# Routed experts of a mixture layer: rows padded to 64 instead of 128 per expert, with pair tiles that hold two experts

## The reference

```python
logits = x @ gate_weight.T                      # 2048 tokens, 8 experts
scores = softmax(logits)
topk_w, topk_idx = top_k(scores, 2)             # two experts per token
gu  = einsum('th,efh->tef', x, gate_up_weights) # 512 -> 2 * 352
act = silu(gu[..., :352]) * gu[..., 352:]
y   = einsum('tef,te,ehf->th', act, combine, down_weights)   # 352 -> 512
y   = y + shared expert (704 wide, all tokens)
```

## Time and profile before

| | |
|---|---|
| time, median of 3 runs | 2844.9 us (2841.21 to 2847.65) |
| profiled execution, its own time | 2848.35 us |
| span of its trace | 2846.3 us |
| mean granted TensorE clock | 0.986 of full speed |
| PE busy (TensorE products) | 2768.9 us, 97% of the span, 13041 records |
| VectorE, ScalarE, GpSimd busy | 1754.0, 1222.0, 607.7 us |
| span of the expert tiles on TensorE | 615.2 to 951.2 us of the span |

### The profile page before, as it was taken

How to read it: one execution, slowest core, us unless ns; L and a number is a source line. 1 busy time by engine, 2 the same in 40 slices (tenths; PEclk the granted TensorE clock), 3 DMA queues, 4 the chain that set the end, 5 groups by cost and what they waited for, 6 DMA issues and landing times. The chain is left out here.

```text
span 2846.3 us, 37554 instructions
## 1 busy us (share of the span) xinstructions
PE 2768.9 (97%) x13041; PEld 1558.3 (55%) x13042; DVE 1754.0 (62%) x4334; ACT 1222.0 (43%) x2268; POOL 607.7 (21%) x669
## 2 busy tenths in 40 slices
PE   8999999989999988999999999999999999999998
PEld 3444444436565445666666656666666665664432
DVE  5767762011111276777877778777787778645986
ACT  4646431012122145456545565455655555342243
POOL 1111101401111312133123331333213332120000
PEclk9999999999999988999999999999999999999999
DMA  3101134031221652011100111001120011227313
GB/s 134 50 1 44 45 114 180 23 122 63 66 66 62 231 219 78 16 46 68 68 30 31 43 63 75 31 31 42 54 85 31 31 42 49 75 75 262 126 48 104
DMA packets 78501, 215.22 MB, mean 76 GB/s; under 512 B 12128, under 2 KB 13056, under 8 KB 69760
## 3 DMA queue, kind: packets, MB, share of 16 engines
q1 hardware_dynamic: 58704, 165.84, 16.0%
q0 software_dynamic: 9264, 28.36, 3.1%
q10 hardware_dynamic: 10368, 18.88, 1.8%
HBM read 156.25 MB, written 56.80 MB: 75 GB/s over the span
## 5 line engine op out<-in xcount | busy, mean ns | idle before, releaser
L2477 DVE SCALAR_TENSOR_TENSOR c_conv<-c_ps_pj,c_conv_t,c_conv 128x511 f32<-128x511 f32 (+2 forms) x450 | 336.2, 747 | 30.0 <-ACT c_conv L2296 19.4
L1961 POOL TENSOR_SCALAR c_gate<-c_gate 128x512 f32<-128x512 f32 x64 | 37.9, 620 | 997.1 <-DVE c_block_L L2510 997.1
L2036 PE MATMUL c_ps_pj<-c_xs,c_w_v 128*128 128x512 f32 x480 | 225.8, 593 | 0.0
L2036 PE MATMUL c_ps_pj<-c_xs,c_w_q 128*128 128x512 f32 x360 | 177.0, 614 | 0.0
L2057 PE MATMUL c_ps_pj<-c_w_g,c_xs 128*128 128x512 f32 x384 | 172.7, 592 | 0.0
L2036 PE MATMUL c_ps_pj<-c_xs,c_w_k 128*128 128x512 f32 x360 | 164.7, 593 | 0.0
L2296 ACT ACTIVATE c_conv<-c_ps_pj,c_conv_t 128x512 f32<-128x512 f32 x150 | 116.6, 777 | 56.3 <-issue 27.6
L1284 DVE TENSOR_TENSOR x_act<-x_hs,x_ps_u 128x352 f32<-128x352 f32 x40 | 20.9, 521 | 191.6 <-ACT x_hs L1269 191.6
L2359 ACT ACTIVATE c_err<-c_negL 32x128 f32<-32x128 f32 x256 | 79.1, 309 | 135.1 <-DVE c_negL L2543 130.4
L2507 DVE TENSOR_TENSOR c_block_X<-c_block_X,c_block_t 128x58 f32<-128x58 f32 (+6 forms) x448 | 117.7, 263 | 15.4
L2504 DVE TENSOR_TENSOR c_block_t<-c_block_L,c_block_X 128x58 f32<-128x58 f32 (+6 forms) x448 | 117.6, 263 | 14.9
(11 more groups left out here) (587 smaller groups left out, 5962.8 us busy)
## 6 DMA issues: line engine op xcount, KB each, us to landing
c_xs<-xt_d SPq DMA_DIRECT2D x16, 1024.0 KB, 4.8
c_G<-cum_d SPq DMA_DIRECT2D x16, 1024.0 KB, 4.6
ot_d<-c_oT ACTq DMA_DIRECT2D x64, 256.0 KB, 2.0
b_w_gu<-in_w_gu SPq DMA_DIRECT2D x8, 1408.0 KB, 21.1
y_slots<-x_y SPq DMA_DIRECT2D x40, 256.0 KB, 2.0
d_x<-x SPq DMA_DIRECT2D x32, 256.0 KB, 3.0
d_switch<-in_switch_w SPq DMA_DIRECT2D x4, 2048.0 KB, 16.9
a_x<-in_x SPq DMA_DIRECT2D x7, 1024.0 KB, 7.0
```

The source lines that it names most:

```text
L2036: mm = e.matmul(bank_of[xb][u][:, :], w["kqv"[u // HG]][:, k, (u % HG) * DH:(u % HG + 1) * DH], xs[xb][:, k, :], start=(k == 0), stop=(k = ...
L2477: e.scalar_tensor_tensor(oc, bank_of[buf][u][:, 0:SEQ - s], conv_t[buf][:, m, h, TAPS - 1 - s:TAPS - s], oc, ALU.mult, ALU.add).then_inc(c ...
```

## The change

Each expert's rows are now padded to a multiple of 64 (HALF). The worst case is then 36 tiles (NS) in place of 40. An expert's whole 128-row tiles come first; the 64-row remainders fill half slots from the end, two to a tile. The last four slots (32 to 35) can thus hold two experts, one in rows 0 to 63 and one in rows 64 to 127. They are computed in places 28, 30, 32 and 34 of the order, with the other tiles between them. In such a **pair tile** each product is two with 64 columns of stationary data: the first with the resident weights of the first expert, the second with weights of the second expert that SyncE loads for this tile (`pair_gu`, 1408 KB, into the space of `kept.w_dn`; `pair_dn`, 768 KB, into the spare end of `s_gu0`). There is one buffer for each, so the next pair's load waits until the products of the last pair have read it. The loads of the shared expert's down weights move from the start of the phase to after the last pair's gate/up products. The loop now covers tiles 1 to 26; tiles 27 to 35 are written out one by one. The routing gets more small VectorE instructions. Cut diff:

```diff
-NS = -(-(2 * NT * P + NE * (P - 1)) // P)
+HALF = P // 2
+NS = -(-((2 * NT * P + NE * (HALF - 1)) // HALF) // 2)
+NW = NS - NE // 2
+PAIRS = {NS - 2 * (NS - s): s for s in range(NW, NS)}
...
-            e.tensor_scalar(padded[:, :], count_upto[:, :, NT - 1], float(P - 1), None, ALU.add).then_inc(route, 1)
+            e.tensor_scalar(padded[:, :], count_upto[:, :, NT - 1], float(HALF - 1), None, ALU.add).then_inc(route, 1)
...
+            (halves_i, halves, odd, odd_ends, odd_base twice, odd_shift: seven [128, 8] instructions
+             before psum_read; slot_of, one [128, 128] instruction, goes)
...
+            (after acts(of_batch(0, 4)): four [128, 128] instructions, then for rt.expert
+             2 scans, 2 odd_no, beyond, 2 x passed, 2 x reduce over [128, 504], 4 small ones
+             in place of 1 scan, 1 passed, 1 reduce over [128, 280], 1 small one)
...
         def tiles(e, each):
             each(0, 0, 0)
-            with e.Fori(0, NS // 2 - 1) as p:
+            with e.Fori(0, first_pair // 2 - 1) as p:
                 each(p * 2 + 1, 1, p)
                 each(p * 2 + 2, 0, p + 1)
-            each(NS - 1, 1, NS // 2 - 1)
+            for t in range(first_pair - 1, NS):
+                each(t, t % 2, t // 2)
...
             def store(t, par, half):
                 e.wait_ge(y_copied, t + 3)
                 stand(e, pr.waits_passed)
-                e.dma_start(io["y_slots"][t], y[par][:, :]).then_inc(y_stored[par], 16)
-            for i in range(NSH):
-                e.dma_start(kept.w_dn[:, i], io["w_dn"][NE + i]).then_inc(kept_loaded, 16)
+                e.dma_start(io["y_slots"][slot_at(t)], y[par][:, :]).then_inc(y_stored[par], 16)
+                if is_pair(t) and t < last_pair:
+                    load_pair_dn(t + 2)
+                if is_pair(t + 1):
+                    e.wait_ge(gu_ready, t + 2)
+                    if t + 1 < last_pair:
+                        load_pair_gu(t + 3)
+                    else:
+                        for i in range(NSH):
+                            e.dma_start(kept.w_dn[:, i], io["w_dn"][NE + i]).then_inc(kept_loaded, 16)
+            def second_expert(t):
+                return e.value_load(rt.expert[0:1, 1, SLOTS[t]:SLOTS[t] + 1], min_val=0, max_val=NE - 1)
+            def load_pair_gu(t):
+                e.dma_start(kept.pair_gu, io["w_gu"][bass.ds(second_expert(t), 1)].rearrange("o p k f -> p (o k) f")).then_inc(pair_gu_loaded, 16)
+            load_pair_gu(first_pair)
+            load_pair_dn(first_pair)
             tiles(e, store)
...
             def down(t, par):
+                if is_pair(t):
+                    e.wait_ge(pair_dn_loaded, 16 * (t - first_pair) // 2 + 16)
...
+                    if is_pair(t):
+                        e.matmul(y_ps[par][0:HALF, :], actT[par][0:width, f, 0:HALF], w_dn[0:width, expert, f, :], **ends)
+                        mm = e.matmul(y_ps[par][HALF:P, :], actT[par][0:width, f, HALF:P], kept.pair_dn[0:width, f, :], **ends)
...
             def tile(t, par, half):
                 e.wait_ge(act_done, t + 1)
+                if is_pair(t):
+                    e.wait_ge(pair_gu_loaded, 16 * (t - first_pair) // 2 + 16)
                 for k in range(KD):
+                    for bank, lo in ((g_ps[par], 0), (u_ps[par], FE)):
+                        if is_pair(t):
+                            e.matmul(bank[0:HALF, 0:FE], xT[par][:, k, 0:HALF], w_gu[:, expert, k, lo:lo + FE], **ends)
+                            mm = e.matmul(bank[HALF:P, 0:FE], xT[par][:, k, HALF:P], kept.pair_gu[:, k, lo:lo + FE], **ends)
+                        else:
+                            mm = e.matmul(bank[:, 0:FE], xT[par][:, k, :], w_gu[:, expert, k, lo:lo + FE], **ends)
```

More of the change, by code:

```diff
@@ L37 @@
 NX = NE + NSH
-NS = -(-(2 * NT * P + NE * (P - 1)) // P)
+HALF = P // 2
+NS = -(-((2 * NT * P + NE * (HALF - 1)) // HALF) // 2)
+NW = NS - NE // 2
+PAIRS = {NS - 2 * (NS - s): s for s in range(NW, NS)}
+SLOTS = [t for t in range(NS - 2 * (NS - NW))]
+for t in range(NS - 2 * (NS - NW), NS):
+    SLOTS.append(PAIRS[t] if t in PAIRS else (t + NS - 2 * (NS - NW) - 1) // 2)
 NH = 16
@@ L807, in __init__ @@
         self.token = sb("token", [P, NS], U32)
-        self.expert = sb("expert", [1, NS], I32)
+        self.expert = sb("expert", [1, 2, NS], I32)
 class KeptShared:
@@ L819, in __init__ @@
         self.acts = tiles
+        flat = tiles[:, NB * KD - NSH * len(FT):, :].rearrange("p t d -> p (t d)")
+        self.pair_gu = flat[:, 0:KD * 2 * FE].rearrange("p (k f) -> p k f", k=KD)
+        spare = s_gu0[:, :, :].rearrange("p k f -> p (k f)")[:, len(KEPT) * SEQ:len(KEPT) * SEQ + len(FT) * DM]
+        self.pair_dn = spare.rearrange("p (f d) -> p f d", f=len(FT))
     def act(self, b, f):
@@ L1094, in _ @@
             e.wait_ge(route, m + 6)
+            e.tensor_copy(halves[:, :], halves_i[:, :]).then_inc(route, 1)
+            e.wait_ge(route, m + 7)
             e.tensor_tensor_scan(ends[:, :], con["ones"][:, 0:NE], tiles[:, :], 0.0, ALU.mult, ALU.add).then_inc(route, 1)
-            e.wait_ge(route, m + 7)
+            e.wait_ge(route, m + 8)
+            e.scalar_tensor_tensor(odd[:, :], tiles[:, :], -2.0, halves[:, :], ALU.mult, ALU.add).then_inc(route, 1)
+            e.wait_ge(route, m + 9)
@@ L1097, in _ @@
             e.tensor_tensor(base[:, :], ends[:, :], tiles[:, :], ALU.subtract).then_inc(route, 1)
[L1098 to L1102, removed]
+            e.wait_ge(route, m + 10)
@@ L1103, in _ @@
+            e.tensor_tensor(t["score"][:, :, :], count[:, :, :].rearrange("p x n -> p n x"), earlier, ALU.add).then_inc(psum_read, 1)
             acts(of_batch(0, 4))
+            over_tokens = lambda a: a[:, :].unsqueeze(1).to_broadcast(shape)
             e.wait_ge(psum_read, 1)
-            m = of_choice(slot_f, t["score"][:, :, :], m + 9)
+            e.scalar_tensor_tensor(t["key"][:, :, :], t["score"][:, :, :], 1.0 / P, over_tokens(tiles), ALU.mult, ALU.is_ge).then_inc(route, 1)
+            e.wait_ge(route, m + 16)
@@ L1117, in _ @@
             e.tensor_copy(at[:, :, :], at_f[:, :, :]).then_inc(placed, 1)
[L1119 to L1122, removed]
+            for h in range(2):
+                e.tensor_tensor_scan(tile_no[:, h, :], con["ones"][:, 0:NS], con["ones"][:, 0:NS], 0.0, ALU.mult, ALU.add).then_inc(route, 1)
@@ L1123, in _ @@
             e.wait_ge(route, m + 7)
-            e.tensor_reduce(expert_f[:, :], passed[:, :, :], AX.X, ALU.add).then_inc(route, 1)
-            e.wait_ge(route, m + 8)
-            e.tensor_copy(rt.expert[:, :], expert_f[0:1, :]).then_inc(route, 1)
+            for h in range(2):
+                e.tensor_scalar(odd_no[:, h, :], tile_no[:, h, :], -2.0, float(2 * NS + 2 - h), ALU.mult, ALU.add).then_inc(route, 1)
+            slots_of = lambda a: a[:, :, :].rearrange("p h t -> p (h t)")
+            by_slot = [P, 2 * NS, NE - 1]
@@ L1208, in gather @@
                                      bass.IndirectOffsetOnAxis(one_token[par][:, :], 0)).then_inc(x_loaded[par], 16)
-            with e.Fori(0, NS // 2 - 1) as p:
+            with e.Fori(0, first_pair // 2 - 1) as p:
                 gather(p * 2 + 2, 0, p + 1)
                 gather(p * 2 + 3, 1, p + 1)
+            for t in range(first_pair, NS):
+                gather(t, t % 2, t // 2)
         @block.tensor
```

63 lines of the change are left out of this document (53 added, 10 removed).

## The result

The changed kernel takes 2816.8 us (median of 4 runs, 2814.1 to 2818.0) beside 2846.3 us of the kernel before on the same chip (2841.2 to 2848.7): a ratio of 0.9895 with a 95% interval of 0.9879 to 0.9910. That is 29.5 us less. The profiled execution took 2816.4 us; its span is 2814.7.

The account below looks back on a forecast made before the run. The prediction took TensorE alone to bound the expert phase. Its terms -32.3 + 1.2 + 1.0 = -30.1 us gave 2818.2 for the profiled execution and 2815 for the median, range 2810 to 2826.

Parts of the forecast that it names:

- What bounds: Expert phase: TensorE alone sets the time, busy 299.04 of 299.04 us at full clock, 8.08 us per tile.
- step 1: Expert phase: four fewer tiles at 8.08 us each save 32.3 us.
- Step 2: Four pair tiles: the two column halves run at once, losing 0.15 us per stretch, +1.2 us in all.
- Step 3: Second expert's gate/up loads before tiles 30, 32 and 34: waits of 0.3 us each, +1 us.
- Step 4: Start of the expert phase: TensorE's 5.44 us wait for down weights in tile 1 stays unchanged, 0.
- Step 5: Shared down weights loaded at the end of the phase: covered by the last tile, landing 5 us early, 0.
- Step 6: Routing: extra small VectorE instructions move `psum_read` 1.1 us later but stay covered by TensorE's work, 0.
- Step 7: Tiles written out behind the loop: no added idle time, 0; other end +4 us.
- Partial overlap in the stream: Pair tiles: all paired work takes 1.01 us per 0.86, four tiles cost 5.0 us more, 2818.6; chance 0.14.
- Slow loads: Pair weight loads take 11.2 us; three waits with half clock behind cost 21.7 us, 2835.5; chance 0.05.
- No overlap: Pair tiles: the halves run one after the other, +29.2 us, 2842, no measurable change; chance 0.05.
- the slower side: Pair tiles: no overlap plus 0.15 us per product, 42.4 us for four against 32.3 saved, 2855; chance 0.03.

Follow-up runs that it names:

- before_36_tiles: The kernel before the change with 36 of its 40 tiles computed and four small stores filling the missing results; 2804.7 us, ratio 0.9875 to the kernel before.
- second_half_left_out: The changed kernel with only the first product of each sum kept for the second half of a pair tile (3 of 11); 2820.4 us, ratio 0.9910.
- first_pair_loads_later: The changed kernel with the first pair's two loads issued behind the first tile's store, not behind the down-weight loads; 2808.5 us, ratio 0.9886.
- kept_loads_last: The changed kernel with the shared expert's down weights loaded behind the last store instead of in tile 35; 2815.5 us, ratio 0.9911.
- gu_load_later: The changed kernel with the second expert's gate/up load for pairs 30, 32 and 34 waiting one tile's gate/up product longer; 2829.0 us, ratio 0.9954.
- halves_apart: The changed kernel with all first-half products of a pair tile's stretch ahead of all second-half products; 2834.4 us, ratio 0.9951.
- the last experiment: The changed kernel with tile 0's down product moved from tile 1 to tile 2, behind tile 2's own gate/up product; 2803.9 us, ratio 0.9879.
- changed_again: The changed kernel run once more, unaltered, on a second chip; 2809.7 us, ratio 0.9890 to the kernel before.
- two_by_two: The changed kernel with gate and up of the first half, then of the second, for each input chunk; 2815.3 us, ratio 0.9894.

## Why the prediction was right

Forecast 2815.0, measured 2816.8: within the range, and by the path that was forecast. Its sum of -30.1 stands against -30.34 in the expert phase, but that this is so close is luck: two of its terms were off by 1 us each, the halves too cheap and the loads too dear, and cancelled.

- **What bounds, and step 1** held: -32.3 predicted, -32.27 measured by before_36_tiles. A full tile is still 8.08 to 8.09 us.
- **Step 2** had the mechanism right and the size wrong. "0.15 us for each of the two stretches" should have been 0.3: 2.4 us in all and not 1.2. The 0.15 inside the stretch was right (4.89 - 4.73 and 2.73 - 2.58, to 0.01). What failed was reading the price from the first half product to the first product behind them. The way in lies before that start. The earlier trace rows showed it: the eight full records ahead of L2812 take 2757.14 - 2753.38 = 3.76 us, where a stream takes 4 x 0.86 = 3.44, and I spread those 0.32 over the products as "what surrounds them". Record by record 0.10 of it lies behind the first of the eight and 0.23 between the last and the first half product (2756.48 to 2757.14 for 0.43): the way in. The sentence that the 0.15 "holds whatever that change of form costs" is thus wrong. The Trainium skill's rule (TensorEngine Tiling, Key Properties: changing the tiling mode drains the engine) fits what second_half_left_out shows, a price at the edges of a stretch that doesn't depend on how much the second half does; it was too small to speak against the change.
- **Step 3**: 0.3 us each predicted, none in the first trace, 0.24 to 0.46 once per phase in three others, about 0.1 on average. The issue 1.9 us into the tile was 1.66, the landing "near 6.0" was 5.8 to 7.1 where a trace has it, the longest ones at tile 30, and the 8.2 us until the need were 8.47, as the down product in halves gives the load more time. So the landing was put right; the earlier issue and the later need are what hid the load, with less than 1 us left.
- **Step 4**: 0 predicted; 5.44 became 5.55, and first_pair_loads_later shows that the pair's loads are no part of it. The six down records behind the wait took 4.67 in place of 5.09. Tile 1 and what it waits for take 15.82 us in place of 16.13. The end of the phase is 0.10 shorter than in the kernel before, halves set aside (14.74 for 14.84, as in before_36_tiles). That closes the sum: -32.33 + 2.4 - 0.3 - 0.1 = -30.3.
- **Step 5**: 0 predicted and found. The two loads are issued at 908.69 and 909.84, 14.1 and 13.0 us before the next phase, and the second landed after 6.1, 6.9 us early. The next phase starts with the same 3.24 us before its first product in both kernels. "The cover is the last tile" is what kept_loads_last shows (+5.3).
- **Step 6**: hidden. The row that answers to the earlier trace rows is the one below; `phase_moe_shared` starts 1.35 us earlier in this trace, so the instruction moved 0.25 us later against it and not 1.1, and TensorE's down product, which waits for it, starts 3.9 us after it:

```profile
464.30 0.36 DVE L1124 TENSOR_TENSOR b_score<-b_count,b_ps_y 128x128 f32<-128x128 f32 x1
468.23 4.03 PE L992 MATMUL b_ps_y<-b_s_dn,b_act 96*128 96x512 f32 x9
```

- **Step 7**: 0, as the steps of 8.08 up to tile 27 and the busy 58.40 of 58.40 us behind it show.
- **The rivals.** Partial overlap in the stream falls: its price would go with the length, and the price is 0.15 inside a stretch of three products and of eight. The shortfall that the Trainium skill gives for three column tiles (TensorE: Matmul & The Clock Gate, Measured speedup vs the span model: 2.38 of 3) is not seen with two: 32 records in 4.89 us against 4.73 for 16 make 1.93. Slow loads did not come, but gu_load_later shows that the rival had its mechanism right, the half clock included, and was one gate/up product's delay away. No overlap would have cost 7.3 us a pair; halves_apart, with four records of overlap left in each stretch, costs 4.5. For the slower side a price per product was needed, and the products cost none.

The median is 1.8 us over the forecast. The kernel before took 2846.3 us in the runs beside the changed one, and 2846.3 - 30.1 is 2816.2: the sum itself was right to about 0.6.

## What to carry to other kernels

Two products in the two halves of TensorE's columns cost as much as one when they are issued alternately or in blocks of four records in turn; the price is 0.3 us for each stretch in halves, so make the stretches few and long. Read such a price from the last full product before to the first one after, not from the first half product on. When TensorE is the bound, a wait of some us costs more than its length, since the clock is low behind it (here 12.1 us of waits cost 19.8): put work whose operands are there in front of the wait, as the last experiment did. And reckon a load to its landing, not to the end of its data (5.9 against 5.3 us in changed_again).

## What the runs showed that I had not expected

- TensorE began products of the other column half while three records of the first half, earlier in the program, were still to start (halves_apart, 896.21). Blocks of four in turn lose only 0.05 us a tile (two_by_two).
- Leaving out all but the first products of the second half saves nothing (8.29 and 8.47 us as before): the 0.3 us are paid for the form, not for the work.
- Behind waits of 4.67 and 4.06 us the granted clock was at half for 6.0 us of products, behind one of 3.39 for 3.3 us, and the three waits of 12.1 us cost 19.8.
- A load of 1408 KB in the same place of the order landed after 5.8 to 7.1 us; in changed_again after 5.94 for one pair and 7.0 for another.
